# An attention block on one core: the reciprocals' broadcast one slot later, O in two buffers and first in GpSimd's slot

## The chip, the cores and the metric

The kernel runs on one core of a Trainium2 chip. The metric is the device time of one execution in microseconds; runs of a kernel are compared by their medians.

## The reference

x has 16 sequences of 256 rows and 256 columns, the context 16 of 256 rows and 192 columns, all float32. One layer is computed:

```
h = layernorm(x);  x = attention(h, h)   + x      # 16 heads of 64
h = layernorm(x);  x = attention(h, ctx) + x      # keys and values from ctx
h = layernorm(x);  p = h @ ff_w1 + b1;  x = (p[:, :1024] * gelu(p[:, 1024:])) @ ff_w2 + b2 + x
attention: softmax(q k^T / 8) v for each head, then @ wo + bo
```

## The kernel before

All matrix products split each float32 operand into a high and a low part and add three products. Attention is cut into slots. A slot is one pair of heads of one sequence: 8 slots for a sequence (`pair` 0 to 7), 16 sequences, two attentions (self, then cross), so 256 slots (`ATT`), and after them the feed-forward part. The work is a pipeline written by hand: every engine runs its own program, a loop over slots c, and in each turn does steps that belong to different slots. Semaphores count finished slots (`a.pl_o`, `a.dve_ad` and so on), and each engine runs strictly in its written order.

In its turn c TensorE does: the scores S of slot c (lines 260 and 261, from the tile RING), the transposes of the probabilities of slot c-1 (L272), the queries and keys of slot c+2 into QKB (L299), the output projection WOP of slot c-3 (L313, waits for `pl_o`, the split O), the values of slot c+1 (L333), probabilities times values PVB of slot c-1 (L348, the last in the turn; it waits for the values' split `pl_v`).

VectorE in turn c: the row maximum of slot c (L471), reciprocals of slot c-1's denominators and their transpose into RDT (L480, L482), the sum of PVB and LP into ON for slot c-2 (L496), the low part of the probabilities (L506), a copy VF of the values of c+1 (L513), the low part of the queries and keys of c+2 (L527, counts `dve_lo`). Once in eight slots other steps lie between: layernorm statistics (L429, pair 0), their aggregate (L435, pair 1), the normalization (L441, pair 2), all between L513 and L527, and the residual sum (L489, pair 3) before L496. ScalarE copies the other half of PVB to LP (L385) and computes the exponentials.

SyncE issues the DMAs. `copy_ring(k)` waits for `dve_lo` of slot k and issues four copies inside SBUF into RING, which the scores of slot k need. `save_den(s)` writes the reciprocals of slot s to a tensor in DRAM (L924), and `spread_den(s)` reads them back in two DMAs as a broadcast to 64 partitions each, into RB (L933); it first waits until what `save_den(s)` wrote has landed. The order of a turn is save_den(c-1), spread_den(c-1), copy_ring(c+2), then now and then loads of weights (L886), of context (L897, L898) or of x, and stores of x.

GpSimd in turn c: the split of the values of slot c (L608, L610), now and then small layernorm steps, splits and weights (`pool_weights`), and last O of slot c-2: ON times RB (L627), its high part (L630), its low part (L632, counts `pl_o`). ON has one buffer, RB and OT have two.

Of the kernel before, what the change touches and what calls it, by code (L numbers as in the profile page):

```python
# [5 lines left out]
F32 = mybir.dt.float32  # L6
F32R = mybir.dt.float32r
ACT = mybir.ActivationFunctionType
ALU = mybir.AluOpType
# [62 lines left out]
def block_kernel(nc, x, ctxt, ln1_g, ln1_b, ln2_g, ln2_b, ln3_g, ln3_b, sa_wq, sa_wk, sa_wv, sa_wo,  # L72
                 sa_bo, ca_wq, ca_wk, ca_wv, ca_wo, ca_bo, ff_w1, ff_b1, ff_w2, ff_b2, out):
    ctx = ExitStack()
    with ctx:
        def sb(name, shape, dt=F32):
            return ctx.enter_context(nc.sbuf_tensor(name, shape, dt))
# [20 lines left out]
        CX = sb("CX", [P, TT, S])  # L98
        RB = sb("RB", [P, 2, S])
        VF = sb("VF", [P, S])  # L100
        LP = sb("LP", [P, S])
        ON = sb("ON", [P, 1, S])
        OT = sb("OT", [P, 2, 2, TT * P], F32R)
        STG = sb("STG", [P, CH])
        IDN = sb("IDN", [P, P])
# [270 lines left out]
        def act_slot(e, sl):  # L376
            c = sl.c
            seq, pair = divmod(c, PAIRS)

            if sl.has(c - 2):  # L380
                s = c - 2
                sl.wait(e, a.pe_pv, s + 1)
                sl.wait(e, a.dve_ad, s)
                for i in range(2):
                    last = e.activation(LP[OWN[i], :], PVB[OTHER[i], i * S:(i + 1) * S], ACT.Copy)  # L385
                last.then_inc(a.act_lp, 1)

            if sl.has(c - 1):
                s = c - 1
                sl.wait(e, a.pe_t, s + 1)  # L390
                sl.wait(e, a.pe_pv, s)
                e.activation(PH[:, :], PTB[:, :, :].rearrange("p i n -> p (i n)"), ACT.Copy) \  # L392
                    .then_inc(a.act_ph, 1)

            if c >= 0 and sl.has(PAIRS * (seq + 1)):
                if pair in (3, 4):
                    act_gain_bias(e, sl, seq + 1, pair - 3)
                if pair in (1, 2) and seq + 1 >= B:
                    act_ctx(e, sl, seq + 1, pair - 1)

            def exponentials(i):

                for qt in range(TT):
                    j = i * TT + qt
                    last = e.activation(PT[:, c % 2, j * S:(j + 1) * S], S1[:, i, qt * S:(qt + 1) * S],  # L405
                                        ACT.Exp, bias=NM[:, j:j + 1], accum_out=DEN[:, c % 2, j:j + 1])
                last.then_inc(a.act_exp, 1)

            if sl.has(c):
                sl.wait(e, a.dve_nm, c + 1)  # L410
                sl.wait(e, a.pe_t, c - 1)
                sl.wait(e, a.dve_rc, c - 1)
                exponentials(0)

            if sl.has(c + 2):
                k = c + 2
                sl.wait(e, a.pe_qk, k + 1)
                if k > 1:
                    await_ring(e, k - 2)
                e.activation(QKS[:, k % 2, 0:2, :], QKB[:, :].rearrange("p (u s) -> p u s", u=2), ACT.Copy) \  # L420
                    .then_inc(a.act_hi, 1)

            if sl.has(c):
                exponentials(1)
# [39 lines left out]
        def dve_slot(e, sl):  # L464
            c = sl.c
            seq, pair = divmod(c, PAIRS)
            prepares = c >= 0 and sl.has(PAIRS * (seq + 1))

            if sl.has(c):
                sl.wait(e, a.pe_s, c + 1)  # L470
                e.tensor_reduce(NM[:, :].rearrange("p (i t) -> p i t", t=TT),  # L471
                                S1[:, :, :].rearrange("p i (t s) -> p i t s", t=TT),
                                AX.X, ALU.max, negate=True).then_inc(a.dve_nm, 1)

            if sl.has(c - 1):
                s = c - 1
                sl.wait(e, a.act_exp, 2 * s + 2)
                if s > 1:
                    e.wait_ge(d_ds[(s - 2) % 4], 16 * ((s - 2) // 4 + 1))
                e.reciprocal(RDEN[:, 0:4], DEN[:, s % 2, :]).then_inc(a.dve_rc, 1)  # L480
                sl.wait(e, a.dve_rc, s + 1)
                e.transpose(RDT[:, s % 2, :], RDEN[:, :]).then_inc(a.dve_rt, 1)  # L482

            if pair == 3 and c > PAIRS:
                n = seq - 1
                sl.wait(e, a.pe_wo, PAIRS * seq)
                sl.wait(e, a.pl_xb, seq)
                cols = sl.x_cols(n)
                e.tensor_tensor(XR[:, cols], WOP[:, :], XR[:, cols], ALU.add).then_inc(a.dve_xo, 1)  # L489

            if sl.has(c - 2):
                s = c - 2
                sl.wait(e, a.act_lp, s + 1)
                sl.wait(e, a.pl_o, s)
                for i in range(2):
                    last = e.tensor_tensor(ON[OWN[i], 0, :], PVB[OWN[i], i * S:(i + 1) * S], LP[OWN[i], :], ALU.add)  # L496
                last.then_inc(a.dve_ad, 1)

            if prepares and pair in (1, 2) and seq + 1 >= B:
                dve_ctx(e, sl, seq + 1, pair - 1)  # L500

            if sl.has(c - 1):
                s = c - 1
                sl.wait(e, a.act_ph, s + 1)
                sl.wait(e, a.pe_pv, s)
                e.tensor_tensor(PL[:, :], PTB[:, :, :].rearrange("p i n -> p (i n)"), PH[:, :].bitcast(F32),  # L506
                                ALU.subtract).then_inc(a.dve_pl, 1)

            if sl.has(c + 1):
                v = c + 1  # L510
                sl.wait(e, a.pe_v, v + 1)
                sl.wait(e, a.pl_v, v)
                e.tensor_copy(VF[:, :], VB[:, 0:S]).then_inc(a.dve_vf, 1)  # L513

            if prepares:
                if pair == 0:
                    dve_await_x(e, sl, seq + 1)
                    dve_stats(e, sl, a, seq + 1)
                if pair == 1:
                    dve_aggregate(e, sl, a, seq + 1)  # L520
                if pair == 2:
                    dve_normalize(e, sl, a, seq + 1)

            if sl.has(c + 2):
                k = c + 2
                sl.wait(e, a.act_hi, k + 1)
                e.tensor_tensor(QKS[:, k % 2, 2:4, :], QKB[:, :].rearrange("p (u s) -> p u s", u=2),  # L527
                                QKS[:, k % 2, 0:2, :].bitcast(F32), ALU.subtract).then_inc(a.dve_lo, 1)
# [70 lines left out]
        def pool_slot(e, sl):  # L599
            c = sl.c  # L600
            seq, pair = divmod(c, PAIRS)
            prepares = c >= 0 and sl.has(PAIRS * (seq + 1))

            if sl.has(c):
                sl.wait(e, a.dve_vf, c + 1)
                sl.wait(e, a.pe_pv, c - c % 2 - 2)
                v = VF[:, :].rearrange("p (g h d) -> p g h d", g=2, d=DH)
                e.tensor_copy(v_part(c, 0), v).then_inc(a.pl_vh, 1)  # L608
                sl.wait(e, a.pl_vh, c + 1)
                e.tensor_tensor(v_part(c, 1), v, v_part(c, 0).bitcast(F32), ALU.subtract).then_inc(a.pl_v, 1)  # L610

            if prepares:
                if pair == 1:
                    pool_rstd(e, sl, a, seq + 1)
                if pair == 3:
                    if seq + 1 == B:
                        e.wait_ge(d_bo, 32)
                    pool_add_bias(e, sl, a, seq + 1)
                if pair in (4, 5):
                    pool_split_h(e, sl, seq + 1, pair - 4)  # L620
            pool_weights(e, c)

            if sl.has(c - 2):
                s = c - 2
                sl.wait(e, a.dve_ad, s + 1)
                e.wait_ge(d_rb[s % 2], 32 * (s // 2 + 1))
                e.tensor_tensor(ON[:, 0, :], ON[:, 0, :], RB[:, s % 2, :], ALU.mult).then_inc(a.pl_or, 1)  # L627
                sl.wait(e, a.pl_or, s + 1)
                sl.wait(e, a.pe_wo, s - 1)
                e.tensor_copy(OT[:, s % 2, 0, :], ON[:, 0, :]).then_inc(a.pl_oh, 1)  # L630
                sl.wait(e, a.pl_oh, s + 1)
                e.tensor_tensor(OT[:, s % 2, 1, :], ON[:, 0, :], OT[:, s % 2, 0, :].bitcast(F32),  # L632
                                ALU.subtract).then_inc(a.pl_o, 1)


        NCK = B // 2
# [217 lines left out]
        def _(e):  # L854
# [145 lines left out]
                    e.wait_ge(a.pl_xb, 2 * B)  # L1000
                    e.dma_start(BOUT[:, :], ff_b2.partition_broadcast(P)).then_inc(d_bo, 16)

            for c in range(-2, ATT + 1):
                if c >= 1:
                    save_den(c - 1)
                    spread_den(c - 1)
                if c + 2 < ATT:
                    copy_ring(c + 2)
                weights(c)
                spill(c)  # L1010
# [13 lines left out]
        def _(e):  # L1024
# [10 lines left out]
            pool_add_bias(e, zero, a, 0)  # L1035
            for p in range(HALF):
                pool_split_wo(e, 0, 1, p)
            run_slots(0, ATT + 2, ATT, lambda sl: pool_attention_slot(e, sl))
            for chunk in range(1, NCK):
                pool_rstd(e, zero_ffn, fs, chunk)  # L1040
                pool_add_bias(e, zero_ffn, fs, chunk)
# [79 lines left out]
```

## Time and profile before

| | |
|---|---|
| Median of 3 runs | 2064.68 us (2061.74 to 4450.36) |
| The profiled execution | 2053.68 us, its span 2051.9 us |
| Busy in the span: TensorE matmul, weight load | 1813.0 us (88%), 1730.0 us (84%) |
| VectorE, ScalarE, GpSimd | 1408.3, 1152.1, 1012.3 us |
| Mean granted TensorE clock | 0.983 of full speed |

The span runs from the first to the last instruction. Busy shares are means over parts of the kernel with different limits; matmuls overlap in the pipeline, so the sum of their idle time is less than what a denser order of them would give back.

### The profile page before, as it was taken

The numbers are of one execution on the slowest core, as the hardware profiler recorded it, in microseconds if no ns is written. First come the engines' busy times: TensorE is split into PE (matmuls) and PEld (weight loads), VectorE is DVE, ScalarE is ACT, GpSimd is POOL, SyncE is SP. The second block draws the span as 40 slices with busy tenths as digits, with TensorE's granted clock in tenths as the row PEclk, the third lists the DMA queues.
The fourth block names the chain that finished last, engine by engine and source line by source line (L and its number), as shares of the span: only waits on it lengthen the run. The fifth ranks groups of instructions, "written<-read, shape, count | busy, mean of one in ns | idle before, by whom it ended". The sixth has DMA issues, their size and how long they took to land.

```text
span 2051.9 us, 42245 instructions
## 1 busy us (share of the span) xinstructions
PE 1813.0 (88%) x13824; PEld 1730.0 (84%) x13824; DVE 1408.3 (69%) x2651; ACT 1152.1 (56%) x3256; POOL 1012.3 (49%) x1727
## 2 busy tenths in 40 slices
PE   4988889888899999988888888898888898899998
PEld 4888888888888889888788888888888888788887
DVE  4766667667777777766667666676777777666664
ACT  3666656656666666656656566666666666321211
POOL 3566655645555555565555655555555554301010
PEclk9999999999999999999999999999999999999999
DMA  6554555555555555555555555555545555101000
GB/s 174 128 146 124 140 132 139 140 131 130 130 127 126 127 127 127 129 127 133 145 137 136 142 132 139 138 130 134 131 122 127 127 131 129 41 21 41 22 21 21
DMA packets 225625, 241.24 MB, mean 118 GB/s; under 512 B 68352, under 2 KB 190592, under 8 KB 225408
## 3 DMA queue, kind: packets, MB, share of 16 engines
q1 hardware_dynamic: 225408, 238.55, 45.9%
q8 instruction: 112, 1.84, 0.4%
q14 instruction: 105, 0.86, 0.1%
HBM read 58.08 MB, written 12.58 MB: 34 GB/s over the span
## 4 chain that ended last, share of the span: by engine, by line
SPq 46%; DMA 31%; PE 16%; issue 5%; DVE 1%; ACT 0%; POOL 0%; DVEq 0%; POOLq 0%
DMA denominators<-RDT 28%; SPq L914 15%; SPq L916 15%; SPq L933 13%; PE S L716 4%; PE PTB L716 4%; PE QKB L729 2%; PE VB L729 2%; DMA RING<-RING 2%; SPq L886 1%; PE QKB L299 1%; SPq L865 1%; PE S L260 1%; PE PTB L272 0%; SPq L897 0%
## 5 line engine op out<-in xcount | busy, mean ns | idle before, releaser
L471 DVE TENSOR_REDUCE NM<-S 128x4 f32<-128x1024 f32 x256 | 313.5, 1225 | 443.6 <-PE S L261 443.6
L392 ACT ACTIVATE PH<-PTB 128x1024 fp32r<-128x1024 f32 x256 | 262.8, 1027 | 542.3 <-PE PTB L272 542.3
L405 ACT ACTIVATE PT<-S,NM 128x256 f32<-128x256 f32 x1024 | 480.9, 487 | 12.1 <-DVE NM L471 12.1
L260 PE MATMUL S<-RING 128*128 128x256 f32 x1024 | 282.4, 308 | 207.8 <-DMA RING<-RING 206.6
L627 POOL TENSOR_TENSOR ON<-ON,RB 128x256 f32<-128x256 f32 x256 | 190.0, 742 | 516.9 <-DVE ON L496 274.5
L260 PEld LDWEIGHTS S<-RING 128*128 128x128 f32 x1024 | 195.8, 191 | 252.5 <-DMA RING<-RING 250.8
L506 DVE TENSOR_TENSOR PL<-PTB,PH 128x1024 fp32r<-128x1024 f32 x256 | 313.4, 1224 | 9.4 <-ACT PH L392 2.1
L272 PE MATMUL PTB<-IDN,PT 128*128 128x128 f32 x2048 | 275.2, 279 | 0.0
L261 PE MATMUL S<-RING 128*128 128x256 f32 x1024 | 259.1, 285 | 0.0
L385 ACT ACTIVATE LP<-PVB 64x256 f32<-64x256 f32 x512 | 194.0, 379 | 101.8 <-PE PVB L348 98.4
L272 PEld LDWEIGHTS PTB<-IDN,PT 128*128 128x128 f32 x2048 | 238.4, 144 | 0.0
L313 PE MATMUL WOP<-WO,OT 128*128 128x256 f32 x1536 | 227.4, 284 | 2.4 <-POOL OT L632 2.3
L405 ACT ACTIVATION_READ_ACCUMULATOR PT<-S,NM 128x1 f32 x1024 | 225.9, 221 | 0.0
L299 PE MATMUL QKB<-HT,WA 128*128 128x256 f32 x1536 | 222.1, 296 | 3.8 <-POOL HT L555 2.4
L496 DVE TENSOR_TENSOR ON<-PVB,LP 64x256 f32<-64x256 f32 x512 | 206.4, 403 | 9.5 <-POOL OT L632 4.4
L313 PEld LDWEIGHTS WOP<-WO,OT 128*128 128x128 f32 x1536 | 202.3, 192 | 3.7 <-POOL OT L632 2.5
L299 PEld LDWEIGHTS QKB<-HT,WA 128*128 128x128 f32 x1536 | 199.0, 198 | 4.5 <-issue 2.7
L632 POOL TENSOR_TENSOR OT<-ON,OT 128x256 fp32r<-128x256 f32 x256 | 188.4, 736 | 20.6
L610 POOL TENSOR_TENSOR VR<-VF,VR 128x256 fp32r<-128x256 f32 x256 | 187.8, 733 | 20.5
L261 PEld LDWEIGHTS S<-RING 128*128 128x128 f32 x1024 | 197.3, 193 | 0.0
L527 DVE TENSOR_TENSOR RING<-QKB,RING 128x512 fp32r<-128x512 f32 x256 | 173.1, 676 | 1.0 <-ACT RING L420 1.0
L534 POOL TENSOR_SCALAR VE<-MV 128x2 f32<-128x2 f32 (+1 forms) x40 | 9.1, 226 | 332.1 <-DVE MV L435 332.1
(106 smaller groups left out, 3283.0 us busy)
## 6 DMA issues: line engine op xcount, KB each, us to landing
RING<-RING SPq DMA_DIRECT2D x512, 192.0 KB, 2.9
RING<-RING SPq DMA_DIRECT2D x512, 128.0 KB, 2.9
RB<-denominators SPq DMA_DIRECT2D x512, 64.0 KB, 2.6
out_dram<-XR SPq DMA_DIRECT2D x32, 256.0 KB, 3.0
XR<-in_x_dram SPq DMA_DIRECT2D x16, 256.0 KB, 3.2
denominators<-RDT SPq DMA_DIRECT2D x256, 16.0 KB
XR<-out_dram SPq DMA_DIRECT2D x16, 256.0 KB, 3.0
CX<-in_ctx_dram SPq DMA_DIRECT2D x16, 192.0 KB, 2.8
```

Source lines behind the costliest of these rows:

```text
L260: e.matmul(o, q, RX[:, c % 2, i, K1, :], start=True, stop=False)
L261: last = e.matmul(o, q, RX[:, c % 2, i, K2, :], start=False, stop=True)
L272: last = e.transpose(PTB[:, i, kt * S + qt * P:kt * S + (qt + 1) * P], PT[:, s % 2, q0:q0 + P], IDN[:, :])
L299: last = e.matmul(QKB[:, m * S:(m + 1) * S], w[:, p * P:(p + 1) * P], act, start=j == 0, stop=j == len(passes) - 1)
L313: last = e.matmul(WOP[:, t * D:(t + 1) * D], OT[:, s % 2, op, t * P:(t + 1) * P], WO[:, p, wp, :], start=p == 0 and t == 0 and j == 0, sto ...
L392: e.activation(PH[:, :], PTB[:, :, :].rearrange("p i n -> p (i n)"), ACT.Copy) \
L405: last = e.activation(PT[:, c % 2, j * S:(j + 1) * S], S1[:, i, qt * S:(qt + 1) * S], ACT.Exp, bias=NM[:, j:j + 1], accum_out=DEN[:, c % 2 ...
L471: e.tensor_reduce(NM[:, :].rearrange("p (i t) -> p i t", t=TT), S1[:, :, :].rearrange("p i (t s) -> p i t s", t=TT), AX.X, ALU.max, negate ...
L506: e.tensor_tensor(PL[:, :], PTB[:, :, :].rearrange("p i n -> p (i n)"), PH[:, :].bitcast(F32), ALU.subtract).then_inc(a.dve_pl, 1)
L914: e.dma_start(RX[OWN[i], r, i, :, :].bitcast(F32), QKS[OWN[i], r, 0:3, :].bitcast(F32)) \
L916: e.dma_start(RX[OTHER[i], r, i, K1:Q1 + 1, :].bitcast(F32), QKS[OWN[i], r, 0:4:3, :].bitcast(F32)) \
L933: e.dma_start(RB[OWN[i], s % 2, :], DS[s % 4, TT * i:TT * (i + 1), :].rearrange("t p -> (t p)").partition_broadcast(P // 2)) \
```

## The change

O takes one slot more on its way. On SyncE `spread_den` is moved ahead of `save_den` and made one turn later, so that it serves slot c-2 in turn c. ON gets two buffers, and LP goes away: ScalarE writes its half into ON itself, and VectorE adds PVB to it in place. The wait for `pl_o` moves from VectorE's sum to ScalarE's copy, and asks for a slot older by two. On GpSimd the three steps of O stand at the head of the turn, for slot c-3, ahead of the values' split of slot c. TensorE's program is the same.

```
-        LP = sb("LP", [P, S])
-        ON = sb("ON", [P, 1, S])
+        ON = sb("ON", [P, 2, S])
@@ ScalarE, has(c - 2)
-                sl.wait(e, a.dve_ad, s)
+                sl.wait(e, a.pl_o, s - 1)
-                    last = e.activation(LP[OWN[i], :], PVB[OTHER[i], i * S:(i + 1) * S], ACT.Copy)
+                    last = e.activation(ON[OWN[i], s % 2, :], PVB[OTHER[i], i * S:(i + 1) * S], ACT.Copy)
@@ VectorE, has(c - 2)
-                sl.wait(e, a.pl_o, s)
-                    last = e.tensor_tensor(ON[OWN[i], 0, :], PVB[OWN[i], i * S:(i + 1) * S], LP[OWN[i], :], ALU.add)
+                    on = ON[OWN[i], s % 2, :]
+                    last = e.tensor_tensor(on, PVB[OWN[i], i * S:(i + 1) * S], on, ALU.add)
@@ GpSimd, first in its turn (before: last, for s = c - 2, with ON[:, 0, :])
+            if sl.has(c - 3):
+                s = c - 3
+                sl.wait(e, a.dve_ad, s + 1)
+                e.wait_ge(d_rb[s % 2], 32 * (s // 2 + 1))
+                e.tensor_tensor(ON[:, s % 2, :], ON[:, s % 2, :], RB[:, s % 2, :], ALU.mult).then_inc(a.pl_or, 1)
+                sl.wait(e, a.pl_or, s + 1)
+                sl.wait(e, a.pe_wo, s - 1)
+                e.tensor_copy(OT[:, s % 2, 0, :], ON[:, s % 2, :]).then_inc(a.pl_oh, 1)
+                sl.wait(e, a.pl_oh, s + 1)
+                e.tensor_tensor(OT[:, s % 2, 1, :], ON[:, s % 2, :], OT[:, s % 2, 0, :].bitcast(F32),
+                                ALU.subtract).then_inc(a.pl_o, 1)
@@ SyncE
-            for c in range(-2, ATT + 1):
-                if c >= 1:
+            for c in range(-2, ATT + 2):
+                if c >= 2:
+                    spread_den(c - 2)
+                if 1 <= c <= ATT:
                     save_den(c - 1)
-                    spread_den(c - 1)
                 if c + 2 < ATT:
                     copy_ring(c + 2)
@@ GpSimd's loop
-            run_slots(0, ATT + 2, ATT, lambda sl: pool_attention_slot(e, sl))
+            run_slots(0, ATT + 3, ATT, lambda sl: pool_attention_slot(e, sl))
```

## Rows read from the trace of the kernel before

**Rows 1.** Busy time by stretch: self attention, cross attention, feed-forward

```profile
core 0: us, PE busy (x) PEld busy (x) DVE busy (x) ACT busy (x) POOL busy (x), PEclk, DMA share, GB/s
20.00:895.00 875.00, 776.09 (x6218) 753.24 (x6219) 610.10 (x1137) 539.55 (x1569) 493.31 (x844) 0.98 0.53 132
895.00:1770.00 875.00, 757.17 (x5993) 730.26 (x5993) 617.34 (x1177) 548.78 (x1600) 480.30 (x823) 0.98 0.52 132
1770.00:2052.00 282.00, 275.56 (x1601) 243.28 (x1599) 169.32 (x322) 54.74 (x79) 31.82 (x45) 1.00 0.07 23
```

**Rows 2.** The chain that ended last, share of the span by line

```profile
DMA denominators<-RDT 28%; SPq L914 15%; SPq L916 15%; SPq L933 13%; PE S L716 4%; PE PTB L716 4%; PE QKB L729 2%; PE VB L729 2%; DMA RING<-RING 2%; SPq L886 1%; PE QKB L299 1%; SPq L865 1%; PE S L260 1%; PE PTB L272 0%; SPq L897 0%
```

**Rows 3.** Waits of SyncE's queue, 60 to 1740 us: total, times, longest

```profile
SPq L933 <- DMA denominators<-RDT: 444.2, 249, 3.2
```

**Rows 4.** Timeline of SyncE, one turn: start us, us

```profile
1002.08 0.57 SPq L924 DMA_DIRECT2D denominators<-RDT  x1
...
1004.42 1.13 SPq L933 DMA_DIRECT2D RB<-denominators  x2
...
1005.64 0.55 SPq L914 DMA_DIRECT2D RING<-RING  x1
...
1007.57 0.62 SPq L916 DMA_DIRECT2D RING<-RING  x1
...
1008.93 0.57 SPq L924 DMA_DIRECT2D denominators<-RDT  x1
```

**Rows 5.** Timeline of the same turn, TensorE and GpSimd, idle before in brackets

```profile
1004.16 0.39 PE L260 MATMUL S<-RING 128*128 128x256 f32 x1 [1.17 <-DMA RING<-RING]
...
1007.91 0.74 POOL L627 TENSOR_TENSOR ON<-ON,RB 128x256 f32<-128x256 f32 x1 [3.25 <-DMA RB<-denominators]
...
1009.19 0.74 POOL L632 TENSOR_TENSOR OT<-ON,OT 128x256 fp32r<-128x256 f32 x1
...
1010.55 0.39 PE L260 MATMUL S<-RING 128*128 128x256 f32 x1 [0.71 <-DMA RING<-RING]
```

**Rows 6.** Timeline of a slot of self attention without a wait

```profile
455.73 0.28 PE L260 MATMUL S<-RING 128*128 128x256 f32 x1
...
459.00 0.88 PE L313 MATMUL WOP<-WO,OT 128*128 128x256 f32 x6
...
460.64 0.43 DVE L513 COPY VF<-VB 128x256 f32<-128x256 f32 x1 [0.20 <-PE VB L333]
...
460.98 0.68 DVE L527 TENSOR_TENSOR RING<-QKB,RING 128x512 fp32r<-128x512 f32 x1
...
461.40 0.28 PE L260 MATMUL S<-RING 128*128 128x256 f32 x1
```

**Rows 7.** Timeline of TensorE, a slot of cross attention

```profile
892.05 0.39 PE L260 MATMUL S<-RING 128*128 128x256 f32 x1 [0.72 <-DMA RING<-RING]
...
897.09 0.64 PE L348 MATMUL PVB<-PL,VR 128*128 128x256 f32 x4
```

**Rows 8.** Instructions of one line: count, min/median/max ns, first and last start

```profile
L260 PE MATMUL S<-RING x1024: 274/283/584, 32.5 to 1757.5; 128*128 128x256 f32 x171
...
L914 SPq DMA_DIRECT2D RING<-RING x498: 477/597/1595, 61.0 to 1739.9; - x166
...
L441 DVE TENSOR_SCALAR XN<-XR,MV,RSTD x62: 402/474/960, 103.9 to 1737.8; 128x256 f32<-128x256 f32 x62
```

**Rows 9.** Timeline of SyncE after the last ring copies

```profile
1759.50 0.56 SPq L924 DMA_DIRECT2D denominators<-RDT  x1
...
1761.48 1.09 SPq L933 DMA_DIRECT2D RB<-denominators  x2
```

**Rows 10.** VectorE's groups, 60 to 880 us: busy us, mean ns, idle before

```profile
L489 DVE TENSOR_TENSOR XR<-WOP,XR 128x512 f32<-128x512 f32 x15 | 9.7, 649 | 0.0
L429 DVE BATCH_NORM_STATS2 ST<-XR 128x6 f32<-128x256 f32 x30 | 11.1, 414 | 0.0
L435 DVE BATCH_NORM_AGGREGATE MV<-ST 128x2 f32<-128x6 f32 x30 | 3.6, 160 | 0.0
```

**Rows 11.** Timeline of SyncE, a load of weights in two issues

```profile
902.77 1.32 SPq L886 DMA_DIRECT2D STG<-in_L_xattn_ca_wo_dram  x2
```

More of the change, by code:

```diff
@@ L621, in pool_slot @@
             pool_weights(e, c)
[L623 to L633, printed above, removed]
         NCK = B // 2
```

## Prediction

> **What bounds the kernel now.** I first read the busy time by stretch [rows 1]. The feed-forward stretch keeps TensorE at 275.56 of 282.00 us, and the change doesn't touch it; there is nothing to win there. In the two attentions TensorE is busy 776.09 + 757.17 = 1533 of 1750 us and no other engine more than 70%, so the loss lies there. The chain that ended last says who holds the attention up: 28% of the span is the way of the denominators' write, some 45% are issues of SyncE, TensorE's attention lines a few per cent [rows 2]. SyncE's own waits give the rest: its broadcast read L933 waited 444.2 us in 249 turns for the write L924 to land [rows 3]. One turn shows why. The write starts at 1002.08, the read at 1004.42, the first ring copy at 1005.64, the last at 1007.57, lasting 0.62 [rows 4]. That is 2.34 of waiting and issuing, 1.22 for the reads, 2.55 for the copies, 0.05 to the next: 6.16 us for the shortest turn, while TensorE stands before its scores each slot until the ring copies land (1.17 and 0.71 us here) [rows 5]. Scores run from 32.5 to 1757.5 us, so 1725 / 255 = 6.76 us is the mean slot [rows 8]: the shortest turn plus what loads, stores and slow issues add. The bound is SyncE's turn.
>
> What is the next bound? A slot where the ring was there in time took TensorE 461.40 - 455.73 = 5.67 us in self attention [rows 6], and VectorE, ScalarE and GpSimd kept up. Matmuls start 0.12 apart (six last 0.88, four 0.64) [rows 6, 7]. In cross attention the last four of a slot start 5.04 after the first; with 4 x 0.12, less the 0.11 by which the first one is longer after an idle engine, that is 5.41 [rows 7].
>
> **The change part by part.**
>
> *The read moved out of SyncE's wait.* Each turn loses the stay between write and read: the write's 0.57 of issue remains, 2.34 - 0.57 = 1.77 us go. When turn c+1 comes to its read, the write of slot c-1 was issued ahead of four copies that take 2.55 [rows 4], more than the 2.34 it needed to land; that wait is gone, not moved. SyncE's turn becomes 6.16 - 1.77 = 4.4 us, and 0.6 to 1.3 more where it loads or stores. It is below 5.67 and stops being the bound.
>
> *The ring copies.* They now start as soon as `dve_lo` counts. In the free slot the low part ends at 460.98 + 0.68 = 461.66, which is 5.93 after the slot's start [rows 6]. The last copy is issued 1.93 after the first and TensorE's scores start 1010.55 - 1007.57 = 2.98 after that [rows 4, 5]. So the scores of slot c+2 could start at 5.93 + 4.91 = 10.84, against 11.34 for two TensorE slots in self attention and 10.82 in cross. The ring is just in time.
>
> *O one turn later, read behind the copies.* This is the new ring of waits. The values' matmuls and WOP stand ahead of VF on TensorE, VF ahead of the low part, the low part ahead of SyncE's copies, the copies ahead of the read of slot c-1, and that read ahead of O of slot c-1, which GpSimd does at the head of turn c+2 and for which WOP waits. Over two slots it sums to: WOP to VF 1.64; VF to the end of the low part 1.02 [rows 6]; copies 2.55 + 0.05 [rows 4]; read issued to O started 1007.91 - 1004.42 = 3.49 [rows 4, 5]; O 1009.19 + 0.74 - 1007.91 = 2.02 [rows 5]; 0.1 for two handovers. That is 10.87. Before, the read went into a queue that had been drained; now it follows the copies at once. The small write shows what this costs: 2.34 behind the copies, 1.98 with none ahead [rows 4, 9]. I add 0.36: 11.23 us. In cross attention one matmul fewer lies in it: 11.11. Two TensorE slots are 11.34 and 10.82. So self attention stays at TensorE's 5.67 a slot, cross attention goes to 11.11 / 2 = 5.56, and neither has room for what comes once in a sequence.
>
> *What comes once in a sequence.* It lies in that loop and is paid, apart from a slack of 4 x 0.11 in self attention. Two loops run interleaved, over even and odd slots; a stall of TensorE serves both, so the longer counts. In the even one: statistics 2 x 0.414 [rows 10], normalization 2 x 0.474 [rows 8], 1.78 together. The odd one has the aggregate 2 x 0.16 and the residual sum 0.65, 0.97, which is covered [rows 10]. The loads of weights, two issues of 1.32 together in 6 of 16 sequences [rows 11], with 0.36 of queue: 0.65 on average. Issues that last up to 1.6 instead of 0.6 [rows 8]: 0.5 a sequence, an estimate. In cross attention also the load of context, by the nearest row 1.32 + 0.36, and the context's low part, as short as VF's 0.43. Self: 2.93 - 0.44 = 2.5. Cross: 5.0.
>
> *ON in two buffers, LP gone, waits for an older slot.* The instructions have the same count and size. VectorE's wait for `pl_o` goes; ScalarE's new one asks for the O of two slots earlier, done a slot before in the order above. Behind it on ScalarE stand the exponentials; nothing reaches them as long as O is not over a slot late. I count both at nothing. If that cover failed, ScalarE's chain would move by O's 2.02.
>
> *GpSimd's new order.* The values' split, as long as O's last two steps (about 1.2 us), now stands behind O and its read. O ends at 10.87 + 0.36 less two slots before WOP is due, so at about 3.2 after the slot's start (WOP starts 459.00 - 455.73 = 3.27 in [rows 6]); the split is then done at 4.4 to 4.5, before VF at 4.91. For PVB it is due at about 4.5: no cost, or 0.1 in every second slot, 13 us at the most. GpSimd is busy 974 of 1750 us [rows 1], 3.8 a slot, and has room.
>
> *The sum.* Self attention: 16 x (8 x 5.67 + 2.5 + 0.5), the 0.5 being four transposes for the next sequence at 0.12, is 774. Cross: 16 x (8 x 5.56 + 5.0) is 792. Together 1566 instead of 256 x 6.76 = 1731: 165 us less. The profiled execution took 2053.7; 2053.7 - 165 = 1889. The median of the runs shown lies 11 us above it and the lower run 8; I take 1885, since some of the extras will overlap.
>
> **Where the notes on the chip bear on it.** TensorE's matmul rows leave 1750 - 1533 = 217 us idle in attention, the weight loads 1750 - 753.24 - 730.26 = 267, my slots 288 (below) [rows 1]. The Trainium skill (Perfetto Trace Analysis, Identifying the Most-Contended Engine) holds busy matmul time to be a bad measure and the weight loads' share a good one; by that rule the most to be had is 267 us, a time of 1787, and the slots bear the rule out. The normalization takes 402 to 960 ns with a median of 474 [rows 8]; if all 62 went to 960 it would cost 62 x 0.49 = 30 us, 1915 in place of 1885. The Trainium skill (SBUF — State Buffer, Who interferes with whom) says that such a VectorE instruction and a GpSimd one shut each other out for their whole length; the spread in the row agrees with that. The normalization stands at the end of a slot and O is moved to its head, so I expect no more such meetings than now.
>
> **The rivals.**
>
> *TensorE alone bounds (1766 to 1830).* If the read lands no later than before, or the extras overlap, slots go at 5.67 and 5.41: 128 x 5.67 + 128 x 5.41 = 1418, and 6 pairs of transposes a sequence at 0.24 are 23, together 1441; 1731 - 1441 = 290 less, 1764. For: the free slot [rows 6]. Against: it was free only because the copies had been issued during a longer slot.
>
> *The transfers crowd (1950 to 2010).* The 16 DMA engines are busy 53% at 6.76 us a slot [rows 1], 3.58 us of each; at 5.6 that is 64%. If landing behind the copies costs 1.4 us rather than 0.36, both attentions go by the loop, 12.2 / 2 = 6.1: some 256 x 0.5 = 128 us given back, less the slack: about 1990. Against: 2.34 against 1.98 [rows 4, 9].
>
> *A new wait of the old size (within 2%).* WOP waits for O, O for the read, for as long as the scores waited for the ring. The loop would have to be 2 x 6.76 = 13.5, 2.3 more than I sum. The same time would show if SyncE still waited for the write, against which the 2.55 of copies ahead of it speak.
>
> *Slower.* The values' split, VF and all of SyncE's turn stand behind the read at the head of GpSimd's turn. The mechanism decides from a landing 2.3 us later than I take; were a read to take the 3.49 twice over, the loop is 14.7, the slot 7.4, and the time 2053.7 + 256 x 0.6 = 2205. No row shows such a read.
>
> **How the numbers follow.** The forecast, 1830 to 1950, gets 0.62; TensorE alone 0.22; crowded transfers 0.07; the old size 0.05; slower 0.04. The likeliest is 1885. The range 1790 to 1950 leaves out the lower part of the first rival and the last three, together about 0.2. Differences within 2%, some 41 us, count as no change. Faster 0.91, same 0.05, slower 0.04.
>
> **What would show it.** SyncE's wait of L933 for L924 is gone (from 444.2 to a few us), and L914 waits for VectorE's L527 instead. TensorE's idle time moves from L260 alone to L260 and L313, the latter behind GpSimd's L632, and falls to 100 us or so in attention. GpSimd's multiply waits for RB in most slots and starts about 1.2 after the scores. Slots of 5.7 in self attention, 5.6 in cross, longer at pairs 0, 2 and 4. The granted clock rises from 0.98 to about 1. I am wrong if landing times behind the copies grow, if GpSimd's split holds PVB up, or if ring copies go late more often than summed.

## The result, and the profile after

The changed kernel takes 1874.61 us (median of 4 runs, 1870.25 to 1879.44), the kernel before 2064.89; the ratio is 0.908, with a 95% interval of 0.905 to 0.911. One of the runs of before took 4450 us, which nothing on record explains; the ratio leaves it out. The profiled execution has a span of 1872.8 us.

The busy time by stretch of the changed kernel, self attention, cross attention and feed-forward, answers [rows 1]:

```profile
20.00:805.00 785.00, 747.67 (x6152) 734.00 (x6153) 604.54 (x1125) 533.37 (x1556) 486.07 (x833) 0.99 0.60 146
805.00:1590.00 785.00, 744.04 (x6057) 724.12 (x6056) 624.56 (x1186) 551.83 (x1613) 485.46 (x834) 0.99 0.60 148
1590.00:1873.00 283.00, 275.85 (x1603) 243.44 (x1601) 170.18 (x323) 55.81 (x80) 31.78 (x45) 0.99 0.07 23
```

The feed-forward part is as long as it was (283 against 282 us). The two attentions take 1570 us instead of 1750, and TensorE stands idle for 78 of them instead of 217. VectorE, ScalarE and GpSimd are busy for the same time as before: no work went away, only waiting. TensorE's own busy time fell too, from 1533 to 1492 us, for as many matmuls (12209, 12211 before): a matmul right after a wait shows a longer row, 0.39 us in [rows 5] against 0.28 in [rows 6], and there are fewer waits now.

The chain that ended last, by line, answers [rows 2] (SPq is SyncE's queue, PEld below is TensorE's weight load; the line numbers are those of the changed kernel: most are one lower than before, and O's L627 and L632 are now L607 and L612):

```profile
PE QKB L298 9%; DMA RB<-denominators 8%; PE WOP L312 8%; PE VB L332 6%; PE PVB L347 6%; PE PTB L271 6%; SPq L913 5%; PE PTB L715 5%; PE S L715 5%; SPq L915 5%; PE S L259 4%; PE S L260 3%; DMA RING<-RING 3%; PE QKB L728 2%; PE VB L728 2%
```

The write of the denominators, 28% of the chain before, is gone. What stands there now is TensorE's own work, and for 8% the read into RB. The waits say the same. First SyncE's queue, 60 to 1560 us, which answers [rows 3]; then the other engines, same stretch (total, times, longest):

```profile
SPq L913 <- DVE RING L526: 253.0, 202, 4.6
```

```profile
POOL ON L607 <- DMA RB<-denominators: 447.8, 214, 4.8
...
DVE VF L512 <- PE VB L332: 89.2, 157, 4.2
PEld WOP L312 <- POOL OT L612: 58.8, 70, 3.1
PE WOP L312 <- POOL OT L612: 43.8, 49, 2.9
...
PE S L259 <- DMA RING<-RING: 13.8, 28, 0.9
```

SyncE no longer waits for the write in this stretch (4.3 us are left in the whole span). It waits for VectorE's low part, which is what an engine with time to spare does. GpSimd's multiply waits for RB 448 us in all, yet it costs TensorE only 44 us: most of this waiting lies beside TensorE's other work. The scores' wait for the ring is down to 14 us.

One turn of SyncE with the O that it feeds, in the timeline of the changed kernel, answers [rows 4, 5]:

```profile
533.49 0.50 SPq L913 DMA_DIRECT2D RING<-RING  x1
...
536.08 1.20 SPq L932 DMA_DIRECT2D RB<-denominators  x2
...
537.38 0.59 SPq L923 DMA_DIRECT2D denominators<-RDT  x1
...
539.45 0.73 POOL L607 TENSOR_TENSOR ON<-ON,RB 128x256 f32<-128x256 f32 x1 [0.30 <-DMA RB<-denominators]
...
540.72 0.74 POOL L612 TENSOR_TENSOR OT<-ON,OT 128x256 fp32r<-128x256 f32 x1
...
541.54 0.95 PE L312 MATMUL WOP<-WO,OT 128*128 128x256 f32 x6
```

Read issued to O started is 3.37 us, O takes 2.01, and WOP follows 0.08 later. By the starts of all such turns the 3.37 is typical: the median from a read's issue to the multiply is 3.38 in the 193 turns with no load or store ahead of the read. The read is issued 2.59 after the first copy. With 1.64 + 1.02 from [rows 6] and 0.1 the two-slot loop of the prediction is 10.73 us; it was put at 11.23.

All scores of the changed kernel, the line that gives the mean slot:

```profile
L259 PE MATMUL S<-RING x1024: 277/283/583, 33.1 to 1578.1; 128*128 128x256 f32 x171
```

(1578.1 - 33.1) / 255 = 6.06 us, against 6.76 [rows 8]. By the starts of L259 it is 6.07 in self attention and 6.04 in cross.

### The profile page after: what moved, and what is told of

It reads as the page before. It is cut to its first block, busy times and chain, and to the rows that moved or that the text cites. A ratio compares the mean times of both kernels' runs of the same rounds, so it can differ in the third digit from the quotient of the medians.

```text
span 1872.8 us, 41989 instructions
## 1 busy us (share of the span) xinstructions
PE 1771.8 (95%) x13824; PEld 1704.8 (91%) x13824; DVE 1410.2 (75%) x2651; ACT 1149.7 (61%) x3256; POOL 1010.2 (54%) x1727
## 4 chain that ended last, share of the span: by engine, by line
PE 57%; SPq 13%; DMA 12%; DVE 7%; POOL 6%; issue 4%; ACT 0%; POOLq 0%; DVEq 0%; ACTq 0%
PE QKB L298 9%; DMA RB<-denominators 8%; PE WOP L312 8%; PE VB L332 6%; PE PVB L347 6%; PE PTB L271 6%; SPq L913 5%; PE PTB L715 5%; PE S L715 5%; SPq L915 5%; PE S L259 4%; PE S L260 3%; DMA RING<-RING 3%; PE QKB L728 2%; PE VB L728 2%
## 5 line engine op out<-in xcount | busy, mean ns | idle before, releaser
L607 POOL TENSOR_TENSOR ON<-ON,RB 128x256 f32<-128x256 f32 x256 | 188.2, 735 | 463.4 <-DMA RB<-denominators 458.1
L384 ACT ACTIVATE ON<-PVB 64x256 f32<-64x256 f32 x512 | 193.9, 379 | 163.8 <-PE PVB L347 160.4
L259 PE MATMUL S<-RING 128*128 128x256 f32 x1024 | 265.6, 292 | 25.8 <-DMA RING<-RING 24.7
L312 PE MATMUL WOP<-WO,OT 128*128 128x256 f32 x1536 | 239.0, 292 | 47.3 <-POOL OT L612 46.0
L271 PE MATMUL PTB<-IDN,PT 128*128 128x128 f32 x2048 | 265.2, 273 | 0.0
L312 PEld LDWEIGHTS WOP<-WO,OT 128*128 128x128 f32 x1536 | 201.2, 191 | 66.4 <-POOL OT L612 61.3
L260 PE MATMUL S<-RING 128*128 128x256 f32 x1024 | 257.5, 284 | 0.0
L259 PEld LDWEIGHTS S<-RING 128*128 128x128 f32 x1024 | 196.4, 192 | 37.4 <-DMA RING<-RING 35.1
L271 PEld LDWEIGHTS PTB<-IDN,PT 128*128 128x128 f32 x2048 | 229.9, 140 | 0.0
L298 PE MATMUL QKB<-HT,WA 128*128 128x256 f32 x1536 | 216.3, 291 | 3.8 <-POOL HT L554 2.4
L495 DVE TENSOR_TENSOR ON<-PVB,ON 64x256 f32<-64x256 f32 x512 | 206.1, 402 | 5.6 <-ACT ON L384 2.1
L612 POOL TENSOR_TENSOR OT<-ON,OT 128x256 fp32r<-128x256 f32 x256 | 188.2, 735 | 20.5
L298 PEld LDWEIGHTS QKB<-HT,WA 128*128 128x128 f32 x1536 | 193.3, 192 | 4.5 <-issue 2.7
L512 DVE COPY VF<-VB 128x256 f32<-128x256 f32 x256 | 108.2, 423 | 95.6 <-PE VB L332 94.5
```

Of the source, the lines that this page charges most:

```text
L259: e.matmul(o, q, RX[:, c % 2, i, K1, :], start=True, stop=False)
L260: last = e.matmul(o, q, RX[:, c % 2, i, K2, :], start=False, stop=True)
L271: last = e.transpose(PTB[:, i, kt * S + qt * P:kt * S + (qt + 1) * P], PT[:, s % 2, q0:q0 + P], IDN[:, :])
L298: last = e.matmul(QKB[:, m * S:(m + 1) * S], w[:, p * P:(p + 1) * P], act, start=j == 0, stop=j == len(passes) - 1)
L312: last = e.matmul(WOP[:, t * D:(t + 1) * D], OT[:, s % 2, op, t * P:(t + 1) * P], WO[:, p, wp, :], start=p == 0 and t == 0 and j == 0, sto ...
L384: last = e.activation(ON[OWN[i], s % 2, :], PVB[OTHER[i], i * S:(i + 1) * S], ACT.Copy)
```

## The experiments

Each kernel ran beside the kernel before on the same chip; differences between experiments are taken from the ratios.

**E1, SyncE's order alone.** The kernel before, ON with one buffer, LP kept, and in SyncE's loop:

```
-            for c in range(-2, ATT + 1):
-                if c >= 1:
+            for c in range(-2, ATT + 2):
+                if c >= 2:
+                    spread_den(c - 2)
+                if 1 <= c <= ATT:
                     save_den(c - 1)
-                    spread_den(c - 1)
```

> The kernel before with SyncE's order alone changed; ON keeps one buffer, LP stays, GpSimd's text stays. My theory: the gain lies in SyncE's order, so nearly all of it comes. The one buffer adds a wait: VectorE's sum of slot s waits for O of slot s-1, which ends about 1.0 + 2.0 = 3.0 us after a slot's start, against 2.6 where the sum would start; the loop from O's end through the sum, the low part of the probabilities, VF, the low part of the queries (3.15), copies 2.6, read 3.4, O 2.0 is 11.15 us over two slots, less than two TensorE slots in self attention (11.34), more than in cross (10.84). So 1880 to 1900 us. Rival, that the second buffer carries the gain: about 2065, as before.

Measured: 1913.05 us, ratio 0.928 (0.926 to 0.930). The order brings 7.2% of the 9.2%. The rest, some 40 us, needs the second buffer, more than the 5 to 25 that I expected. The wait of E1 that the changed kernel doesn't have:

```profile
DVE ON L496 <- POOL OT L632: 115.0, 144, 3.6
```

VectorE stands in its sum until O of the slot before is out of ON, 144 times, 0.8 us each, and everything down to the ring copies stands behind it. I had allowed for 0.4 us and for the loop's nominal length only, not for the steps that come once in a sequence, which find no slack left. No run separates this last point, but the starts of the scores agree with it: of the 35 us by which E1's slots are longer in sum, pairs 1 and 2 hold 21.

**E2, the buffers alone.** The changed kernel with SyncE's loop as it was (the diff of E1 reversed).

> The changed kernel with SyncE's old order: write, read of the same slot, copies. GpSimd's instructions stand in the same order as in both kernels, only ON has two buffers. My theory: SyncE's turn of 6.16 us and its extras bound again, so 2055 to 2070 us and a wait of L932 for the write of about 440 us. Rival, that the second buffer carries a part: 2040 or less.

Measured: 2064.6 us, ratio 1.000 (0.998 to 1.002). The row of SyncE's waits:

```profile
SPq L932 <- DMA denominators<-RDT: 456.9, 256, 3.4
```

This is as expected: with the old order the second buffer is worth nothing. E1 and E2 together show an interaction: 0 for the buffers, 149 us for the order, 190 for both.

There is no experiment on GpSimd's order, for there is nothing to undo. I compared the two kernels' GpSimd instructions in order, and they are the same. The last step of turn c (O of c-2), followed by the first of turn c+1 (the values' split), is the same list as O of (c+1)-3 moved to the head of turn c+1. Only two steps for the feed-forward part, near the end, have changed places with an O (11 of 1730 positions differ). So O stands where it stood in GpSimd's order, and WOP still serves slot c-3; what moved by a slot is the read.

**E3, one issue more ahead of the read.** The changed kernel, with the two calls exchanged:

```
-                if c >= 2:
-                    spread_den(c - 2)
                 if 1 <= c <= ATT:
                     save_den(c - 1)
+                if c >= 2:
+                    spread_den(c - 2)
```

> The changed kernel with the broadcast read issued behind the write of the same turn instead of ahead of it: one issue of 0.64 us more in the loop from WOP through VF, copies and the read to O, and in nothing else. My theory of the two-slot loop (10.7 us now, by the trace after): 11.4 us, equal to two slots of self attention and 0.5 more than two of cross; cross attention alone pays 0.25 us a slot, 32 us, and the once-a-sequence steps lose 0.6 of slack every other slot, at most 38 us: 1900 to 1945 us, the idle time before WOP doubled. Rival, that TensorE alone bounds and the read is covered: 1875, as the changed kernel.

Measured: 1928.21 us, ratio 0.935 (0.933 to 0.937), 54 us more for 0.64 us in the loop. The wait for O, whole span:

```profile
PEld WOP L312 <- POOL OT L612: 124.6, 145, 3.9
```

The changed kernel has 61.3 there, so it doubled, as expected. Were TensorE alone the bound, the 0.64 would have been hidden; it wasn't, so the loop through the read binds, and the time lies inside the 1900 to 1945 that I expected from it. The edit does one thing more: the read now also stands behind the write's wait for VectorE's transpose, but in 60 to 1610 us that wait is only 5.1 us in all.

**E4, the read ahead of the loads.** The changed kernel with

```
-                if c >= 2:
-                    spread_den(c - 2)
-                if 1 <= c <= ATT:
+                if c >= 1:
                     save_den(c - 1)
                 if c + 2 < ATT:
                     copy_ring(c + 2)
+                if c >= 1:
+                    spread_den(c - 1)
```

and the loop's end at `ATT + 1`; the loads and stores (`weights`, `spill`) follow the read.

> The changed kernel with the read issued right behind the turn's ring copies, ahead of the turn's loads and stores, which stood before it. My theory: the stalls before WOP at pair 2 and 6, up to 2.9 us each, come from loads of weights and context that stand ahead of the read in the queue. They go, some 20 to 30 us less: 1845 to 1858 us; WOP's idle time at pair 6 of cross attention falls from 11 us to 2 or less. Rival, that they come from the layernorm steps on VectorE ahead of the low part: 1870 to 1875.

Measured: 1842.59 us, ratio 0.894 (0.892 to 0.896), 30 us less than the changed kernel and a little below my 1845 to 1858. What it removed can be seen in the changed kernel's timeline, where a load of weights stands ahead of a read:

```profile
1016.59 1.25 SPq L885 DMA_DIRECT2D STG<-in_L_xattn_ff_w_dram  x2
...
1017.93 1.18 SPq L932 DMA_DIRECT2D RB<-denominators  x2
...
1023.26 0.72 POOL L607 TENSOR_TENSOR ON<-ON,RB 128x256 f32<-128x256 f32 x1 [3.52 <-DMA RB<-denominators]
...
1025.31 0.98 PE L312 MATMUL WOP<-WO,OT 128*128 128x256 f32 x6 [2.94 <-POOL OT L612]
```

Here O starts 5.33 us after the read's issue instead of 3.37: the load costs its 1.3 us of issue and 2.0 us more behind it, and TensorE stands 2.94 us. This is the worst of 14 reads behind a load of weights; they have 3.85 to 5.33, with a median of 4.08, so 0.7 us more is typical. The 15 reads behind a load of context have a median of 3.29: they pay for its issue (1.27 us) and for nothing else. By slots of cross attention (mean of each pair, us, worked out from the starts of L259; idle time before WOP is the sum over 15 sequences):

```
                     pair 2   pair 6    idle before WOP, pair 2 / pair 6
changed kernel        6.88     6.42        13.7 / 10.1
E4                    6.62     5.71         3.6 /  0.3
E5 (below)            6.41     6.35         7.2 /  8.5
```

The turn at pair 4 loads the context, and the read behind it serves the O that WOP waits for at pair 6. E4 settles it: this stall was the loads'. Pair 2 keeps half a microsecond or more with the loads out of the way.

**E5, layernorm steps behind the low part.** The changed kernel, on VectorE:

```
+            if sl.has(c + 2):
+                ...                      # L526, low part of the queries and keys
             if prepares:
                 ...                      # statistics, aggregate, normalization
-            if sl.has(c + 2):
-                ...
```

> The changed kernel with VectorE's once-a-sequence steps (statistics, aggregate, normalization) behind the low part of the queries (L526) instead of ahead of it, so that SyncE's copies and read don't wait for them. My theory of the two-slot loop: the 0.8 and 0.7 to 1.2 us of pairs 0 and 2 leave the loop; they hold up the row maximum of the next slot instead, which has 0.2 to 0.9 us of idle time ahead of it. 15 to 35 us less than the changed kernel: 1840 to 1860 us. Rival, that what these pairs lose comes from the loads alone: 1870 to 1880.

Measured: 1855.3 us, ratio 0.898 (0.896 to 0.900), 22 us less than the changed kernel. The steps' share is real, and it is another share than the loads': pair 6 stays, pair 2 shrinks.

**E6, both.**

> The read ahead of the loads (as in e4) and the layernorm steps behind the low part (as in e5). If both causes are separate parts of the same loop, what is left above TensorE alone shrinks again: e4's 1843 less another 10 to 30 us, 1813 to 1833. If the two act on the same stalls, 1838 to 1845. TensorE alone would be about 1765.

Measured: 1834.02 us, ratio 0.888 (0.885 to 0.890; E4's is 0.892 to 0.896), a microsecond above my 1813 to 1833. E4 brought 30 and E5 22 us, both together 43: mostly separate, partly the same stalls. This kernel beats the changed one by 2.1 points of the ratio. The idle time before the two waiting lines, 40 to 1530 us of E6:

```profile
PE S L259 <- DMA RING<-RING: 14.0, 33, 1.3
PE WOP L312 <- POOL OT L612: 11.4, 34, 2.6
```

**E7, no write and no read.** The changed kernel, leaving the denominators out: `save_den` and `spread_den` are not called, GpSimd sets RB to ones once, and neither it nor VectorE waits for those DMAs. The outputs are not normalized.

> The changed kernel without the denominators' write and broadcast read: SyncE issues neither, GpSimd multiplies O by a tile of ones that is set once, so the outputs are not normalized. The loop from WOP through the read to O is gone; the ring copies alone tie SyncE to the slot. If the read's loop is what holds the changed kernel above TensorE's own 1765, the time falls far: to 1790 to 1815, the rest being ring copies late behind VectorE's layernorm steps. If the ring copies are the main cause, it stays above 1840. If the changed kernel were bound by TensorE already, 1870 to 1875.

Measured: 1825.22 us, ratio 0.884 (0.882 to 0.886), 50 us less than the changed kernel and 20 less than E4. This lies between my first two cases. The loop through the read is a main cause but not the only one. The run takes out a little more than that loop: SyncE also issues three DMAs fewer in each turn, so its copies have more room.

**E8, as E7, with the layernorm steps behind the low part.** Outputs not normalized either.

> As e7, outputs not normalized, and the layernorm steps behind the low part as in e5. Neither the read's loop nor the late low part is left, so this shows what TensorE needs by itself: by my sum 1441 us of attention, 1765; 1765 to 1785 expected. If it stays above 1800, TensorE's own slots are longer than the free slot, or the ring copies bind in every slot of cross attention.

Measured: 1810.54 us, ratio 0.877 (0.876 to 0.878). My expectation of 1765 to 1785 failed; the clause for a time above 1800 holds. Two slots of cross attention in E8, the first with a late ring:

```profile
905.50 0.28 PE L259 MATMUL S<-RING 128*128 128x256 f32 x1
...
909.73 0.64 PE L347 MATMUL PVB<-PL,VR 128*128 128x256 f32 x4
910.77 0.39 PE L259 MATMUL S<-RING 128*128 128x256 f32 x1 [0.40 <-DMA RING<-RING]
...
916.29 0.28 PE L259 MATMUL S<-RING 128*128 128x256 f32 x1
...
921.72 0.28 PE L259 MATMUL S<-RING 128*128 128x256 f32 x1
```

The free slot of cross attention is there, 921.72 - 916.29 = 5.43 us, as summed. But the last four matmuls of the slot before start at 0.12 each, so the next scores could have started at 909.73 + 0.48 = 910.21; they started at 910.77, 0.56 later, of which the row calls 0.40 idle. The mean slot of E8 stays at (1512.8 - 31.8) / 255 = 5.81 by its row of scores:

```profile
L259 PE MATMUL S<-RING x1024: 274/283/580, 31.8 to 1512.8; 128*128 128x256 f32 x171
```

So ring copies that come late by less than a microsecond are part of what is left. The starts in E8's trace say how large a part. In 240 of the 256 slots the gap ahead of the scores is over the usual 0.12 us by 20 us in sum, the gap ahead of WOP by 10 us; of the rest of the 45 us, 12 are longer gaps inside the scores, WOP and PVB. Of the 20 us, 15 fall on 70 slots in which the issues of the four ring copies took 0.3 us or more over 0.6 each; the other 170 slots have 5. This is a coincidence in one trace that no run has tested, but it names the next suspect: slow issues.

## Why the prediction was right

*The bound and where the gain comes from: right.* SyncE's wait was the bound. E2 keeps the wait and keeps the time; E1 removes the wait alone and gives 149 of 190 us.

*The wait vanishes and isn't moved: right.* No wait of the read for the write in 60 to 1560 us.

*O's start, 1.2 us after the scores: right.* Scores at 538.20, multiply at 539.45; the median of all turns is 1.03.

*The two-slot loop: right as the next bound, mis-sized both ways.* E3 lengthens it by 0.64 us and pays 54 us; E7 takes it away and gains 50. The term of 0.36 us for a read behind the copies was not there: issue to O is 3.37, not 3.85, and the landing time of the read has the same median in both kernels, 2.6 us. The rows of the changed kernel:

```profile
L932 SPq DMA_DIRECT2D RB<-denominators x512: 448/587/1261, 48.2 to 1588.6; - x171
...
DMA to landing us min/median/max: 2.4/2.6/4.6
```

So the nominal loop of 10.73 us leaves 0.6 us of slack in self attention, where 0.11 was counted, and in cross attention, with 10.61, it stays below TensorE's 10.82, where it was put above. What comes now and then was too small in exchange. Behind a load of weights the read loses 0.7 us, not 0.36. The stores and loads of x were left out of the loop's sum; each is an issue of 0.74 us ahead of a read, in 32 turns. Slow issues were put at 0.5 us a sequence; in 240 slots of the changed kernel 77 issues took more than 0.9 us, 55 us above 0.6 each, which is 1.8 a sequence.

In self attention the two errors cancel: 6.05 us a slot predicted (774 / 128), 6.07 measured. In cross attention they don't: 6.19 predicted (792 / 128), 6.04 measured, 19 us in all, about what the loop was put above TensorE there (128 times 0.15). That the number came so near is partly luck in one more way: the sum was taken off the profiled execution of before, which lies 11 us below the median. Between medians 190 us went, where the sum had 165.

*Once-a-sequence steps on VectorE, 28 us an attention (1.78 x 16) before slack: right in kind.* Moving them brought 22 us over both attentions (E5). That is less than was charged, but moved steps still cost something where they stand now, so E5 gives no more than a lower bound for the charge.

*ON in two buffers, counted at nothing: right as a cost, wrong as a worth.* In the old order the two buffers cost nothing (E2). But in the new one a single buffer would have cost 40 us (E1), and the prediction never asked what the new order would be without the second. The sum didn't suffer, for it had no single buffer to charge for.

*GpSimd's new order: misread.* I wrote that the values' split "now stands behind O and its read". It stood there before, one turn's name earlier; the list of instructions is the same. The price of nothing was right, for another reason than the one given.

*The normalization and GpSimd shutting each other out (the Trainium skill, SBUF — State Buffer, Who interferes with whom): as much as before.* Its row is 402/474/960 ns before [rows 8] and in the changed kernel

```profile
L440 DVE TENSOR_SCALAR XN<-XR,MV,RSTD x66: 400/407/910, 5.9 to 1559.4; 128x256 f32<-128x256 f32 x66
```

The median fell, but the sum of the 66 is 34.8 us against 33.6, and 15 of them took over 0.8 us against 10: the cost of 30 us did not come, and the meetings are no fewer. The traces agree with the Trainium skill on this: in both kernels the normalizations of attention with no GpSimd instruction beside them took 401 to 414 ns, and those of over 800 ns ran beside one for 0.7 us or more.

*TensorE alone, 1766 to 1830: not reached by the changed kernel.* E7 (1825) and E8 (1811) fall into this range, but the 1764 that it was summed to is out of reach even for E8: the slots promised 290 us (288 in another place of the prediction), the weight loads' idle time 267, and E8 brought 255. The rest would need ring copies and O that are never late. *Crowded transfers, old size, slower:* nothing of them shows; the median landing of the read stayed at 2.6 us. The granted clock rose from 0.983 to 0.993 of full speed, as said.

## What to carry to other kernels

When a queue's turn contains "write, wait until it landed, read back", give the read to the next turn: the wait then lies under the queue's own work. Look also for the buffer that the new order needs: here the order alone gave 7% of the whole, with the second buffer 9%, and the buffer alone nothing. Then sum the next loop over as many slots as it spans, and put what comes now and then (loads, layernorm steps) behind the instruction that the loop waits for: that gave another 2%. Before pricing a step that is moved from the end of one turn to the head of the next, write out the list of instructions: it may be the same list.

## What the runs showed of the hardware

A small read issued right behind four copies of 128 to 192 KB inside SBUF lands as fast as one issued after the queue had waited for the write (median 2.6 us in both kernels). Behind a weight load of two 256 KB DMAs from DRAM the way from issue to use grew from a median of 3.38 us to 4.08 (14 reads, 5.33 at the most); behind a context load of 192 and 64 KB it did not grow (3.29, 15 reads). The issue of a DMA on SyncE mostly took 0.6 us, but 77 in 240 slots took 0.9 to 2.1. The idle time in a row of TensorE is smaller than what is lost: 0.40 us in the row at 910.77 against 0.56 from the starts.
